# Output phase of a selective-state mixer: where the sums of squares and the next group's first score products stand

## The reference

```python
proj = jnp.einsum('bsd,ed->bse', x, in_proj_w)            # gate, hBC, dt
# hBC: causal convolution of width 4, then SiLU; it splits into hs, Bm, Cm
dt = jnp.clip(jax.nn.softplus(dt + dt_bias), DT_MIN, DT_MAX)
Y_diag = jnp.einsum('bzlhn,bzshn,bhzls,bzshp->bzlhp', Cc, Bc, L, xch)   # L: decays, xch: hs * dt
Y = (Y_diag + Y_off).reshape(b, s, H, P) + hs * D[None, None, :, None]  # one chunk: Y_off is 0
g = y * jax.nn.silu(gate)
gg = g.reshape(b, s, G, INTER // G)              # G = 8 groups of 1024 channels
var = jnp.mean(gg * gg, axis=-1, keepdims=True)
gg = gg * jax.lax.rsqrt(var + EPS)
out = gg.reshape(b, s, INTER) * norm_w
return jnp.einsum('bsi,oi->bso', out, out_proj_w)
```

## Time and profile before

| | us |
|---|---|
| median of 3 runs | 2502.57 (2501.91 to 2503.82) |
| the profiled execution | 2504.92 |
| its span, first to last instruction | 2503.2 |
| TensorE busy | 2453.3 |
| DVE, ACT, GpSimd busy | 1840.4, 1156.9, 1133.5 |

### The profile page before, as it was taken

How to read it: one execution, slowest core, us unless ns; L and a number is a source line. 1 busy time by engine, 2 the same in 40 slices (tenths; PEclk the granted TensorE clock), 3 DMA queues, 4 the chain that set the end, 5 groups by cost and what they waited for, 6 DMA issues and landing times. The chain is left out here.

```text
span 2503.2 us, 39348 instructions
## 1 busy us (share of the span) xinstructions
PE 2453.3 (98%) x14024; PEld 2027.6 (81%) x14024; DVE 1840.4 (74%) x2568; ACT 1156.9 (46%) x2732; POOL 1133.5 (45%) x928
## 2 busy tenths in 40 slices
PE   8999999999999999999999999979999999999999
PEld 5667788888888888888888888778888888888886
DVE  4798995986977968859869769656667666766674
ACT  3544343443343443433434434446567566666551
POOL 5332765545655655555556556633223223223123
PEclk9999999999999999999999999989999999999999
DMA  4100430321412303213213122111011011101100
GB/s 184 60 27 31 163 121 36 122 93 55 147 42 89 122 34 121 98 43 134 93 55 141 49 89 89 59 43 35 26 29 49 18 35 47 28 28 28 55 3 34
DMA packets 71622, 172.64 MB, mean 69 GB/s; under 512 B 9312, under 2 KB 17632, under 8 KB 63008
## 3 DMA queue, kind: packets, MB, share of 16 engines
q1 hardware_dynamic: 64448, 165.37, 19.0%
q10 hardware_dynamic: 7008, 4.98, 0.6%
HBM read 165.08 MB, written 5.24 MB: 68 GB/s over the span
## 5 line engine op out<-in xcount | busy, mean ns | idle before, releaser
L270 PE MATMUL pair<-XH,d_w_hi 128*128 128x512 f32 x1160 | 472.4, 407 | 1.7 <-DVE d_gated L1855 1.7
L271 PE MATMUL pair<-XL,d_w_hi 128*128 128x512 f32 x1160 | 460.3, 397 | 0.0
L272 PE MATMUL pair<-XH,d_w_lo 128*128 128x512 f32 x1160 | 460.0, 397 | 0.0
L1701 POOL TENSOR_TENSOR d_decay<-d_decay,d_cb 128x1024 f32<-128x1024 f32 x128 | 315.4, 2465 | 134.8 <-DVE d_decay L1832 123.6
L1832 DVE TENSOR_TENSOR_SCAN d_decay<-d_decay,m_delta 128x1024 f32<-128x1024 f32 x128 | 360.8, 2819 | 2.2 <-DVE d_dtg L1800 1.3
L1682 POOL TENSOR_TENSOR d_w_lo<-d_w,d_w_hi 128x512 fp32r<-128x512 f32 x144 | 190.9, 1328 | 259.3 <-ACT d_w_hi L1500 258.6
L270 PEld LDWEIGHTS pair<-XH,d_w_hi 128*128 128x128 f32 x1160 | 219.0, 189 | 59.2 <-issue 11.7
L1817 DVE SCALAR_TENSOR_TENSOR d_hs<-pair,d_conv,d_hs 128x1016 f32<-128x1016 f32 (+2 forms) x192 | 242.8, 1265 | 29.3 <-ACT d_hs L1525 24.8
L272 PEld LDWEIGHTS pair<-XH,d_w_lo 128*128 128x128 f32 x1160 | 218.7, 189 | 53.0
L271 PEld LDWEIGHTS pair<-XL,d_w_hi 128*128 128x128 f32 x1160 | 219.1, 189 | 47.4 <-issue 0.2
L1525 ACT ACTIVATE d_hs<-pair,d_conv 128x1024 f32<-128x1024 f32 x64 | 77.1, 1205 | 360.7 <-PE pair L272 360.7
(11 more groups left out here) (305 smaller groups left out, 6121.6 us busy)
## 6 DMA issues: line engine op xcount, KB each, us to landing
d_decay<-token_decays SPq DMA_DIRECT2D x64, 1024.0 KB, 4.9
d_w<-in_L_w_groups SPq DMA_DIRECT2D x144, 256.0 KB, 2.7
e_w<-in_L_w_heads SPq DMA_DIRECT2D x80, 256.0 KB, 2.8
d_wo<-in_L_wo_groups SPq DMA_DIRECT2D x64, 256.0 KB, 4.9
e_ctx<-in_ctx_t SPq DMA_DIRECT2D x8, 512.0 KB, 9.1
context_keys<-k_out SPq DMA_DIRECT2D x9, 256.0 KB, 2.1
X<-in_x SPq DMA_DIRECT2D x8, 256.0 KB, 10.2
b_ctx<-in_ctx SPq DMA_DIRECT2D x8, 256.0 KB, 11.5
```

The costliest lines, as they stand in the source:

```text
L270: pe.matmul(out, wh, xh, start=first, stop=False)
L271: pe.matmul(out, wh, xl, start=False, stop=False)
L272: return pe.matmul(out, wl, xh, start=False, stop=last)
L1701: pool.tensor_tensor(r, r, GM_[:], ALU.mult).then_inc(q["scores"], 1)
```

## The change

In the seven groups that have a next one:

- ssq(0) goes from between the halves of batch 1 to right behind the exact products. ssq(1) and (2) stand behind batch 1, (3) and (4) behind batch 3, (5) and (6) behind batch 5, ssq(7) behind batch 7.
- ACT makes square(1) right behind square(0), ahead of batch 1's high parts, and later squares one batch earlier. DVE makes sum(1) ahead of the mask product, and the later sums one or two batches ahead.
- VAR and RV are made for batch 0, the three pairs and batch 7: five operations of one or two columns on each engine.
- The next group's two score products on GpSimd become four of 512 tokens, behind batches 2 to 5.

```diff
-                            if last_group and b == 0 or not last_group and b == 1 and x == 0:
-                                ssq(0)
                         if b == 0 and not last_group:
                             cb(g + 1)
-                        if b:
-                            ssq(b)
+                        for x in (b,) if last_group or b == 0 else (b, b + 1) if b % 2 and b + 1 < NB else (b,) if b % 2 else ():
+                            ssq(x)
...
                     gated_sq(g, 0)
+                    if not last_group:
+                        gated_sq(g, 1)
                     for b in range(1, NB):
                         gated_hi(g, b, last_group, out_halves(b, last_group))
                         if b == 1 and not last_group:
                             silu(g + 1, 2)
-                        gated_sq(g, b)
+                        gated_sq(g, b if last_group else b + 1)
...
+                def first_scores(g, e, h):
+
+                    if h == 0:
+                        pool.wait_ge(q["cb"], START + g + 1)
+                        pool.wait_ge(q["decay"], START + 2 * g * JT + e + 1)
+                    t = tokens(h)
+                    done = pool.tensor_tensor(R[:, 0, e, t], R[:, 0, e, t], GM_[:, t], ALU.mult)
+                    if h == 1:
+                        done.then_inc(q["scores"], 1)
...
-                        rstd(g, b - 1)
-                        if not last_group and b in (2, 3):
-                            scores(g + 1, 0, b - 2)
+                        rstd(g, b - 1, last_group)
+                        if not last_group and 2 <= b < 6:
+                            first_scores(g + 1, b // 2 - 1, b % 2)
...
+                    if not last_group:
+                        var(0)
+                        sq_sum(g, 2)
+                        add(0)
+                        for b in range(1, NB - 1, 2):
+                            var(b)
+                            sq_sum(g, b + 2)
+                            add(b)
+                            if b + 3 < NB:
+                                sq_sum(g, b + 3)
+                            add(b + 1)
+                        var(NB - 1)
+                        add(NB - 1)
+                        return
...
                     sq_sum(g, 0)
                     if not last_group:
+                        sq_sum(g, 1)
                         cb_mask(g + 1)
                     acc(g, last_group)
```

More of the change, by code:

```diff
@@ L1203, in out_step, with var_of, var_columns @@
             return 2 * x + b if last_group and b < 2 else 2 * b + x
+        NV = NB // 2 + 1
+        def var_of(b, last_group):
+            return b if last_group else (b + 1) // 2
+        def var_columns(b, last_group):
+            return slice(b, b + 1) if last_group or b in (0, NB - 1) else slice(b, b + 2)
         def out_halves(b, last_group):
@@ L1339, in scan @@
                     if j == 0:
-                        pe.wait_ge(q["var"], START + g * NB)
+                        pe.wait_ge(q["var"], START + g * NV)
                     pe.wait_ge(q["scores"], START + 2 * (g * JT + j) + 2)
@@ L1361, in ssq @@
                         pe.wait_ge(q["sq_sum"], START + g * NB + b + 1)
-                        pe.wait_ge(q["var"], START + g * NB + b)
+                        pe.wait_ge(q["var"], START + g * NV + var_of(b, last_group))
                         pe.matmul(c.bank[2][:, 2 * b:2 * b + 2], SQS[:, b % 2, :], m["ONE2"][:], start=True,
@@ L1548, in gated_sq @@
                 def gated_sq(g, b):
+                    if b == NB:
+                        return
                     if b == 0:
@@ L1708, in gated_lo, with rstd @@
                                            GH[:, n % 2, :, :].bitcast(F32), ALU.subtract).then_inc(q["g_lo"], 1)
-                def rstd(g, b):
-                    pool.wait_ge(q["var"], START + g * NB + b + 1)
-                    pool.tensor_tensor(RV[:, b:b + 1], VAR[:, b:b + 1], c.mhalf[:, 0:1], ALU.pow).then_inc(q["rstd"], 1)
+                def rstd(g, b, last_group):
+                    if not last_group and b and b % 2 == 0:
+                        return
+                    t = var_columns(b, last_group)
+                    pool.wait_ge(q["var"], START + g * NV + var_of(b, last_group) + 1)
+                    pool.tensor_tensor(RV[:, t], VAR[:, t], c.mhalf[:, 0:t.stop - t.start], ALU.pow).then_inc(q["rstd"], 1)
                 def group(g, last_group=False):
@@ L1863, in acc, with var, add @@
                 def acc(g, last_group):
+                    def var(b):
+                        t = var_columns(b, last_group)
+                        n = START + g * NV + var_of(b, last_group)
+                        v.wait_ge(q["ssq_ready"], START + g * NB + t.stop)
+                        v.wait_ge(q["rstd"], n)
+                        v.tensor_scalar(VAR[:, t], c.bank[2][:, 0:2 * NB].rearrange("p (b o) -> p b o", o=2)[:, t, 0],
+                                        1.0 / (JT * P), 1e-5, ALU.mult, ALU.add).then_inc(q["var"], 1)
+                    def add(b):
+                        v.wait_ge(q["rstd"], START + g * NV + var_of(b, last_group) + 1)
+                        v.wait_ge(q["out_ready"], START + 2 * g * NB + out_step(b, 1, last_group) + 1)
+                        v.scalar_tensor_tensor(c.X[:, b, :], out_bank(b, last_group)[:, :], RV[:, b:b + 1],
+                                               c.X[:, b, :], ALU.mult, ALU.add).then_inc(q["acc"], 1)
+                    if not last_group:
[11 more added lines that the diff above has]
+                        add(NB - 1)
+                        return
                     for b in range(NB + 1):
@@ L1868, in acc @@
                         if b:
[L1869 to L1873, removed]
+                            add(b - 1)
                             v.wait_ge(q["acc"], START + g * NB + b)
@@ L1877, in acc @@
                             v.bn_aggr(c.moments[:, b - 1, :], c.stats[:, b - 1, :]).then_inc(s.moments, 1)
-                        if last_group and 4 <= b < NB:
+                        if 4 <= b < NB:
                             turned_lo(c, v, s, b - 4, x_bank(b - 4))
                         if b < NB:
[L1881 to L1885, removed]
+                            var(b)
+                        if b >= 2:
                             norm_apply(c, v, s, b - 2)
```

## The result

| | before | changed |
|---|---|---|
| median of 5 runs, us | 2502.57 (2501.91 to 2503.82) | 2545.48 (2544.78 to 2547.13) |
| ratio | | 1.017 (95% interval 1.0158 to 1.0181) |
| profiled execution, us | 2504.92 | 2545.48 |
| its span, us | 2503.2 | 2543.8 |

The change makes the kernel 1.7% slower. The medians differ by 42.9 us, the two profiled executions by 40.6; it is the second number that the trace can explain, as the profiled execution of before lies 2.35 us over its median.

What follows compares the result with a forecast made beforehand. TensorE, busy 2453.3 of 2503.2 us, was taken as the bound. Seven phases' +24.8 us and the clock's 10.5 made 2540.2 us against the profiled execution, 2537.9 against the median; range 2526 to 2546.

Steps and rivals of the forecast that it cites:

- main case: Whole kernel: a stop at ssq(0) with the lower clock behind it, 2538 us, from 2533 to 2542; chance 0.70.
- the rival with the dearer clock: Behind the seven stops: clock costs 2.0 to 2.6 us per stop, 2541 to 2546 us; chance 0.13.
- the sum without the clock: Each of seven phases: 4.60 late, minus 0.14, 0.33 and 0.58, gives 3.55 us lost; +24.8 us in all.
- part 3: Behind the exact products: ssq(0) waits for DVE's mask product, TensorE stands some 4.2 us, batch 1 starts 4.60 us late.
- part 1: Paired ssq on TensorE: four of nine switches between matmul kinds go, 0.33 us per phase gained.
- part 2: Score products in halves on GpSimd, 1.25 us each: TensorE's stop behind batch 2 goes, 0.58 us per phase gained.
- part 4: Behind each of seven stops: clock falls to 1.2 GHz, 1.5 us each, 10.5 us in all.
- upper end of 2.6 us: Clock's price per stop, at most: half of the 5.6 us at the low level behind an earlier stop, less a little.
- The case with the clock up: At ssq(0): the stop is there but the clock stays up or falls once or twice, 2527 us; chance 0.12.
- The faster case: At ssq(0): no stop, as the mask product is through in time; -6.4 us, 2496 us; chance 0.03.

Runs made afterwards that it cites:

- kernels 3 and 4: Changed kernel with DVE's mask product ahead of sum(1): 2527.35 us; changed kernel with ssq(0) back between the halves of batch 1: 2530.87 us.
- kernel 1: Changed kernel plus 17 matmuls, whose result nobody reads, between the exact products and ssq(0): 2532.13 us, ratio 1.0114.
- kernel 5: Changed kernel with the mask product ahead of sum(1) and square(1) behind batch 1's high parts and the SiLU: 2511.44 us, ratio 1.0029.
- kernel 2: Kernel before with only the score products split into four halves: 2499.23 us, ratio 0.9982.
- kernel 6: Changed kernel with mask product first, square(1) behind batch 1's high parts and SiLU, ssq(0) between batch 1's halves: 2508.45 us, ratio 1.0019.

## Why the prediction was right, and where it was off

The forecast was 2538 us (2526 to 2546); measured were 2545.5. Sign and mechanism hold, but the size was too small: the time lies outside the main case (2533 to 2542, chance 0.70), in the rival with the dearer clock (2541 to 2546, chance 0.13), and 0.5 us inside the range. Of the 7.6 us, about 4.6 are the clock's price, 1.3 the sum without the clock (the switches above all, which brought nothing), and 2.3 the difference between the kernel before's profiled execution and its median, which the changed kernel doesn't have; against them stand 0.7 us ahead of the first phase. By its steps:

- **The stop at ssq(0)** (part 3): 4.2 us expected, 4.12 measured, released by the mask product, in each of the seven phases. Each link of the line of four took what the earlier trace rows say. Batch 1's low parts had, as said, no effect while this stop was there; kernels 3 and 4 show that they were the next limit, at 4.86 us.
- **The sum without the clock**: 3.55 us a phase, measured 3.7 (kernel 1). The delay of batch 1 was right, 4.58 us against 4.60 (6.28 us behind the exact products against 1.70). The gains behind it were 0.84 us (kernel 5), not 1.05.
- **The switches** (part 1, 0.33 us): this term failed. TensorE's timeline of the changed kernel, a pair behind batch 1:

```profile
755.98 0.65 PEld L1371 LDWEIGHTS pair<-m_one,d_sq_sum 128*128 128x128 f32 x4
756.54 0.19 PEld L270 LDWEIGHTS pair<-d_wo_hi,d_gated_hi 128*128 128x128 f32 x1
```
```profile
756.21 0.50 PE L1371 MATMUL pair<-m_one,d_sq_sum 128*128 128x2 f32 x4
756.57 0.48 PE L270 MATMUL pair<-d_wo_hi,d_gated_hi 128*128 128x512 f32 x1
```

  The weight loads of a single ssq in the kernel before:

```profile
756.48 0.42 PEld L1363 LDWEIGHTS pair<-m_one,d_sq_sum 128*128 128x128 f32 x2
```

  The pair takes 0.36 us to the next product, where one ssq takes 0.14: the second costs 0.22, all that the first costs with the slower batch behind it (0.14 + 0.08). Two batches and two ssq take 11.44 us either way (756.85 to 768.29 before), and kernel 5 leaves the pairs no gain. I had read the 0.08 us behind an ssq as a switch between two kinds of matmul, to be paid once for each run of them. It is rather a part of what every ssq costs. Why is not shown; the weight loads fit it, as two stand in a row of 0.42 us and four in one of 0.65, and the 0.23 us between them are about the price of the second ssq. I didn't test that with a kernel of its own.
- **The stop behind batch 2** (part 2): gone, as said. A half took 1.30 us, where I took 1.25; kernel 2 gives 0.63 us a phase for it, where I had 0.58.
- **The clock** (part 4): the term that was mis-sized. It fell at all seven stops, as forecast. The Trainium skill, "TensorE: Matmul & The Clock Gate", section "HAM oscillation — how this bites in real kernels", tells of DMA waits of some 3 to 5 us between bursts, behind which the lower clock comes back every time. The changed kernel's stops of 4.12 us agree (seven of seven). The stops of kernels 3 and 4 are shorter than those waits, and the case told there doesn't cover them; five of seven were followed by a fall in each. I took 1.5 us each, 10.5 in all; it was about 1.6 four times and 2.9 three times, 15.1 in all. The 1.54 us from the earlier trace rows were right for the short form. I had held a fall inside the stop to be the cheaper case, since part of it costs nothing. The rows show that it can be the dearer one: where it came 0.4 us or more before the stop's end, the low stretch was twice as long, as in the earlier trace rows at 59.90 behind the 4.5 us stop. That row was in hand and I used it for the range only. My upper end of 2.6 us was below the 2.8 to 3.0 of the long form: at 59.90 more than 1 us of the low stretch lay inside the stop, here 0.9 us at most. What decides between the two forms stays open.
- The seven phases' 26.1 + 15.1 us make 41.2; less the 0.7 us that the changed kernel is ahead when the first phase starts (its exact products start at 384.74, before at 385.42), that is 40.5 of the 40.6 us between the two profiled executions. The other 2.3 us of the medians' difference are spread between executions, which no row explains.

**The rivals.** That the clock costs 2.0 to 2.6 us a stop is what came: 2.2 on the mean. The case with the clock up was made real by kernel 1, at 2532 us with its fillers, where I had given 2527. The faster case, in which the mask product is through in time, fell with the 4.12 us.

## What to carry to other kernels

Before a small operation is moved up on a full, in-order engine, list all its waits, and then the queue in front of each operation that releases it: here the operation that was moved takes 0.14 us, and the wait behind it hung on a line of four on two other engines. Where two waits end close together, removing the longer one wins only their difference (1.2 of 4.1 us here). Of a change in several parts each should be timed alone: the halves gave 4.4 us by themselves, and the pairs won nothing where they caused no wait (kernel 5) and took 1.15 us a phase where ssq(0) no longer did (kernel 6).

## What the runs showed of the hardware

- A stop of TensorE costs more than its length once the clock falls behind it: 1.6 us for a short low stretch (3.4 us), 2.8 to 3.0 us for a long one (6.8 us). In the changed kernel the long one came in the three phases in which the fall began 0.4 to 0.9 us before the stop's end, and not in the one in which it began 0.2 us before.
- Equal stops are not followed by equal clocks in one execution: of seven stops of 2.92 us, five were followed by a fall, and of seven pairs of 1.43 and 1.13 us, five. Stops of 1.43 us alone had none in seven, 4.12 us seven in seven. The stop of 1.7 us in the last group was followed by a fall in the kernel before and by none in the changed one (1606.59 to 1608.30). Which of the equal stops brings the fall is not explained here.
- Putting matmuls whose result nobody reads into a stop kept the clock at 1.00 and made the kernel 13.4 us faster. It is a way to measure the clock's share, and no cure: the kernel is still 28.5 us over before.
- A float32 matmul of two columns costs 0.22 us between three-pass products, alone or in a pair: two batches take 2 x 5.50 us without one and 11.44 us with two.
